# Attention of a decoder layer: the causal steps of all head groups first, then the context steps

## The reference

```
for each of 4 batches:
    x1  = x + mamba(norm(x))                       # a scan over 512 steps, 512 channels, 16 states
    xn  = norm(x1)
    q, k, v = xn Wq, xn Wk, xn Wv                  # 16 heads of 16 channels
    cq, ck, cv = xn Wcq, ctx Wck, ctx Wcv
    y   = softmax(mask(q k^T) / 4) v               # causal: 512 queries, 512 keys
        + softmax(cq ck^T / 4) cv                  # context: 512 queries, 1024 keys
    x2  = x1 + y Wp
    out = x2 + mixture_of_experts(norm(x2))        # 8 experts, 2 of them per token, and a gate
```

## Time and profile before

| | us |
|---|---|
| median of three runs (lowest, highest) | 1807.3 (1805.04, 1811.45) |
| the profiled execution, its own time | 1806.43 |
| its span, first to last instruction | 1804.6 |
| PE busy in the span | 1459.6 (81%) |
| DVE busy | 1285.0 (71%) |
| ACT busy | 818.7 (45%) |
| POOL busy | 645.6 (36%) |
| mean granted TensorE clock | 0.925 of 2.4 GHz |

### The profile page before, as it was taken

How to read it: one execution, slowest core, us unless ns; L and a number is a source line. 1 busy time by engine, 2 the same in 40 slices (tenths; PEclk the granted TensorE clock), 3 DMA queues, 4 the chain that set the end, 5 groups by cost and what they waited for, 6 DMA issues and landing times. The chain is left out here.

```text
span 1804.6 us, 19456 instructions
## 1 busy us (share of the span) xinstructions
PE 1459.6 (81%) x6520; PEld 720.5 (40%) x6520; DVE 1285.0 (71%) x2029; ACT 818.7 (45%) x1586; POOL 645.6 (36%) x630
## 2 busy tenths in 40 slices
PE   5697879995987799877887899945677998589995
PEld 2353522242544232243543222422242223378784
DVE  5998488748996778389985886599948881543324
ACT  3643336756443256664433467453323665222221
POOL 2565341303864322207653322056634021212130
PEclk9899979997999889998998899979997998689998
DMA  4950362003002532021004420030034302157744
GB/s 120 343 159 1 105 138 57 14 13 130 19 1 56 143 67 49 14 94 55 1 10 127 107 58 26 2 132 10 0 95 104 67 26 84 49 160 248 237 153 140
DMA packets 128068, 153.87 MB, mean 85 GB/s; under 512 B 19109, under 2 KB 107694, under 8 KB 125920
## 3 DMA queue, kind: packets, MB, share of 16 engines
q1 hardware_dynamic: 124224, 143.96, 27.5%
q0 software_dynamic: 3744, 8.66, 1.3%
HBM read 102.82 MB, written 50.99 MB: 85 GB/s over the span
## 5 line engine op out<-in xcount | busy, mean ns | idle before, releaser
L170 PE MATMUL PS<-arena 128*32 128x512 f32 (+10 forms) x4150 | 832.0, 450 | 85.0 <-DVE maxs L1849 21.5
L170 PEld LDWEIGHTS PS<-arena 128*32 128x32 f32 (+3 forms) x4150 | 363.9, 128 | 525.4 <-ACT arena L1821 205.6
L1821 ACT ACTIVATE arena<-PS 128x512 f32<-128x512 f32 (+3 forms) x768 | 361.6, 547 | 226.5 <-PE PS L170 225.5
L1404 POOL TENSOR_TENSOR arena<-arena 128x1024 f32<-128x1024 f32 x124 | 292.7, 2362 | 215.6 <-DVE arena L1429 117.1
L1849 DVE TENSOR_REDUCE maxs<-PS 128x1 f32<-128x1024 f32 x256 | 298.0, 1215 | 42.1 <-PE PS L170 41.9
L1429 DVE TENSOR_TENSOR_SCAN arena<-PS,arena 128x1024 f32<-128x1024 f32 x128 | 292.1, 2282 | 0.1
L170 PE MATMUL PS<-arena,ident 128*128 128x512 f32 (+1 forms) x560 | 256.5, 584 | 5.4 <-DVE arena L1438 5.4
L1376 ACT ACTIVATE PS<-arena,A_neg 128x511 f32<-128x511 f32 x256 | 165.9, 681 | 202.8 <-DVE arena L1429 202.6
L1438 DVE TENSOR_TENSOR arena<-arena,PS 128x1024 f32<-128x1024 f32 x128 | 156.3, 1221 | 6.8 <-PE PS L170 2.7
L1565 POOL TENSOR_SCALAR_AFFINE_SELECT arena<-arena 128x128 f32<-128x128 f32 x256 | 73.0, 296 | 235.9 <-ACT arena L1821 232.3
L170 PE MATMUL PS<-bc,bc_sel 96*128 96x512 bf16 x128 | 51.8, 405 | 118.8 <-DVE arena L1438 112.4
(11 more groups left out here) (264 smaller groups left out, 1549.7 us busy)
## 6 DMA issues: line engine op xcount, KB each, us to landing
arena<-in_ew SPq DMA_DIRECT2D x46, 512.0 KB
arena<-stack_parts SPq DMA_DIRECT2D x288, 64.0 KB, 2.3
rows_in<-nil SPq DMA_DIRECT2D x16, 1088.0 KB, 12.6
arena<-b_rows SPq DMA_DIRECT2D x16, 1024.0 KB, 7.7
stack_parts<-arena SPq DMA_DIRECT2D x40, 384.0 KB, 2.6
arena<-stack_parts SPq DMA_DIRECT2D x96, 128.0 KB, 4.3
arena<-rows_in SPq DMA_DIRECT2D x23, 272.0 KB, 5.3
xn<-dens SPq DMA_DIRECT2D x24, 256.0 KB
```

The costliest lines, as they stand in the source:

```text
L170: return nc.tensor.matmul(o, l, r, start=start, stop=stop)
L1404: nc.gpsimd.tensor_tensor(b_sb[i % 2], u[:, 2 * kh:2 * kh + 2, :], Brow[:, n, :].unsqueeze(1).to_broadcast([P, 2, T]), ALU.mult).then_inc( ...
L1821: nc.scalar.activation(probs[(HG * s + h) % NPR][:, 0:N], ring_bank(n)[:, 0:N], ACT.Exp, scale=HD ** -0.5).then_inc(S["ring_read"], 1)
```

## The change

The step order becomes side by side instead of group by group: steps 0 to 15 are the four causal steps of groups 0 to 3, steps 16 to 47 the eight context steps of groups 0 to 3.

- The job list is one list of 96 with the order: 8 causal jobs of group 0, 4 context jobs of group 0, then the causal jobs of groups 1, 2 and 3, the other 12 context jobs of group 0, and the context jobs of groups 1, 2, 3. Sixteen stand ahead of the first step; the table gives 2 or 3 per step up to step 10 and 2 per step from there until the list is empty. `TURNS` is the order of the turns: four causal, four context.
- `project(6)` and `project(7)` move ahead of the first job; they stood between the first jobs.
- Q and K are kept for all four groups (`q_last` is new), and SP loads them early. Loads, maximum rows and stores are written in a new order on SP.
- The causal `values` alternate between banks 6 and 7; so the score ring has two banks (4, 5) up to the first context step, and three from there.
- POOL writes the ones of K[0], K[1], K[2] and KC[0] before `low(2)`, where it wrote K[0] and KC[0]; K[3] and KC[1] before the first mask, KC[2] behind the last.
- The causal sides of all groups are copied to `YT[g]`, their denominators inverted once for all groups behind the parts of context group 1, and multiplied by POOL; the context sides follow group by group in `YX`, each inverted behind the parts of a later group.
- In `entry` the last group has only its context side left: 4 matrix multiplications in `turned_sums` and 4 in `spread_sums`, where 8 and 8 stood.

```diff
-            RING = (4, 5, 7)
-            TILE_BANKS = (0, 1, 6, 7, 4, 5, 6, 7, 6, 7)
+            TILE_BANKS = (0, 1, 6, 7, 4, 5, 6, 7, 4, 5)
+            PAIRED = HG * NG * TT + HG
+            def ring_bank(n):
+                return bank((4, 5)[n % 2] if n < PAIRED else (4, 5, 7)[(n - PAIRED) % 3])
+            def step(s):
+                return (s // TT, CAUSAL, s % TT) if s < NG * TT else \
+                    ((s - NG * TT) // CS, CONTEXT, (s - NG * TT) % CS)
+            TURNS = [(g, side) for side in range(2) for g in range(NG)]
...
-                JOBS_AT = [[0] * TT + [4, 2, 3, 3, 2, 2, 2, 2], [2] * STEPS, [2] * STEPS, [0] * STEPS]
+            JOBS_AT = [2, 2, 2, 3, 3, 2, 2, 2, 2, 3, 3] + [2] * (NSTEP - 11)
...
+                for s in range(NSTEP):
+                    g, side, k = step(s)
+                    if k == 0:
+                        pe.wait_ge(max_rows[g], 16 * 3 * (side + 1))
+                    pending = turned[0] < len(TURNS) and J > last_job(*TURNS[turned[0]])
+                    scores(s, (0, 1))
+                    if pending:
+                        max_rows_out(*TURNS[turned[0]])
+                    elif jobs:
+                        max_job(jobs[0])
+                    scores(s, (2, 3))
+                    if jobs and not pending:
+                        max_job(jobs[1])
+                    if s:
+                        values(s - 1)
+                    for j in jobs if pending else jobs[2:]:
+                        max_job(j)
...
                 def turned_sums():
                     pe.wait_ge(S["pv_copied"], 2 * NG)
-                    for i, y in enumerate(YS[(NG - 1) % 2]):
-                        for t in range(TT):
+                    for t in range(TT):
```

482 lines of the change are left out of this document (251 added, 231 removed).

## The result

The changed kernel takes **1794.8 us** (median of 6 executions, 1793.3 to 1796.3) against 1806.5 for the kernel before: a ratio of 0.9931, interval 0.9921 to 0.9942. Faster, then, by 12 us and not by the 28 that were forecast. Its profiled execution took 1793.6 us with a span of 1791.7, so it is compared with the 1806.4 and 1804.6 of before: -12.9 us of span.

What follows compares the result with a forecast made beforehand. PE and DVE were taken as the busy engines, each setting the pace in places. Start +3.3, exps -7.1 and tail -2.0 gave -5.8 for batches 1 to 3, -10.8 for batch 0: -28.2 from 1806.4, 1778 us, range 1765 to 1790.

Steps and rivals of the forecast that it cites:

- That is 17.8 us: From first job to first exp: reductions, turn, two rest, matrices, scores and exp were summed to 17.8 us.
- The 1.7 us of lower clock: Start of batches 1 to 3: a PE pause of about 3.5 us brings the lower clock, ending projections 1.7 us later.
- batch 1 speaks for all four: Attentions: exps take 147 us in both batches shown, so batch 1's trace was priced for all four.
- the 138.3 us of the sum: First to last exp step: causal block, context steps and turns sum to 138.3 us against 145.4 before, -7.1 us.
- the clock falls once more in the block: Rival, causal block: PE slack brings another lower-clock stretch, 3 to 5 us per batch, 1790 to 1798; chance 0.17.
- First job later by 3.3 us: Start of batches 1 to 3: two more K sets on POOL delay low(2) to (4), loads and first job by 3.3 us.
- Projections 6 and 7 in the gap: Start: PE does projections 6 and 7, 1.88 us each, while the first job waits for its loads, 4.17 us before.
- Causal block 50.3 us: Steps 0 to 15 with 36 jobs: groups of 12.0, 12.3, 13.6 and 11.9 plus 0.5 waiting, 50.3 us.
- The rival on the other side: Rival, steps 0 to 15: PE at 1.2 GHz through the causal block, about 22 us per batch, 1866; chance 0.10.
- A wait of 2.1 us for a stack in step 5: Causal step 5: group 3's Q and K loads queue behind maximum rows, PE waits 2.1 us, bounds 0 and 4.
- Steps of 2.89 and 2.45: Context steps: 2.89 us with two jobs (22 of them), 2.45 without jobs (nine intervals).
- Tail -2.0: Tail: two runs of 16 small matrix multiplications become 8 each, 2.0 us less on PE's way to the projections.

Runs made afterwards that it cites:

- experiment 4: Changed kernel with K[1], K[2] ones rows behind the low parts, rest(8), rest(9) among the first eight jobs, group 3 stacks loaded sooner: 1776.7 us, 0.9851.
- 7: experiment 4 with POOL's ones rows of K[3] moved behind the masks of step 4 and KC[1] behind the last mask: 1780.1 us, 0.9855.
- 11: 10 with three more idle multiplications per batch around the first turn: 1772.5 us, 0.9807.
- 10: 7 with one idle multiplication (result unread) per batch in PE's 1.06 us entry pause: 1773.6 us, 0.9819.
- experiment 3: Changed kernel with SP's loads of Q and K of group 3 issued ahead of the maximum rows of causal group 1: 1791.3 us, 0.9918.
- experiment 1: Changed kernel with POOL's ones rows of K[1] and K[2] set behind the low parts of tiles 2 to 4: 1787.5 us, 0.9912.
- experiment 9: Changed kernel with projections 6 to 9 put back behind jobs 1, 3, 5 and 7, their rest() between the maxima: 1806.8 us, 0.9989.
- Experiment 2: Changed kernel with rest(8) on DVE behind the maxima of jobs 0 to 3 and rest(9) behind jobs 4 and 5: 1798.8 us, 0.9947.
- experiment 13: Changed kernel with idle multiplications (results unread), one in the entry and three around the first turn per batch: 1794.2 us, 0.9918.
- Experiment 12: Kernel before with three idle multiplications (results unread) per batch around the turn of context group 0: 1791.2 us, 0.9917.
- 14: Kernel before with idle multiplications in the entry, around the first turn and at the turn of context group 0: 1801.4 us, 0.9966.
- 5: Changed kernel with one idle multiplication (result unread) per batch in PE's 1.06 us entry pause: 1794.7 us, 0.9925.
- 8: Kernel before with one idle multiplication (result unread) per batch in the entry: 1807.4 us, 1.0000.
- 15: 11 with one more idle multiplication, 384 columns wide, ahead of the multiplications that turn the denominators: 1769.0 us, 0.9799.
- experiment 6: Changed kernel with idle multiplications at four places per batch: entry, the 3.45 us pause, first turn, steps 10 and 11: 1794.7 us, 0.9935.

## Why the prediction was off

**The direction held, and of the mechanisms most; the size did not.** 1794.8 us lies within the 8-in-10 bounds (1757 to 1805) but outside the forecast's own range of 1765 to 1790. 15 us are missing, and two steps of the argument failed.

*The step "That is 17.8 us" (first job to first exp).* It takes 20.4 to 21.3 us, 2.6 to 3.5 us more in each of four batches; in batch 0, whose start was to be 1.7 us shorter, that made it 0.9 longer. In batch 1 (20.75) the pieces of the sum against the trace: the first matrix before the first reduction 1.6 instead of 0.9; eight jobs 6.9 instead of 6.7; turn and parts 1.45 as summed; two `rest` 2.7 instead of 1.5, the chain DVE, ACT, DVE; four context jobs 4.6 as summed; from there to the first exp 3.45 instead of 2.5, at 1.2 GHz. I summed durations of DVE and left out what stands between them. Experiments 4 and 7 confirm the chain: with `rest` moved up the stretch is 18.9 to 19.6 us. Part of the rest is the clock: with idle multiplications around the first turn the stretch is about 1 us shorter (18.2 to 18.4 in 11, 18.8 to 19.5 in 10). The 1.7 us of lower clock that I added to each start fell as forecast in batches 1 and 2 but cost nothing, since the loads landed no sooner (experiment 3). Net: 8 us too short over four starts. Batch 3's start grew by 6.4 us where batch 1's grew by 4.7; there the clock fell sooner. The multiplications by `out_w` took 8.83 us (8.56 in the kernel before, 7.14 in batch 1 of both), the second value tiles 3.78, not 2.52, and PE reached its first job 2.4 us later than in batch 1. PE of batch 3 (`out_w` at 1311.37):
```profile
1337.27 3.78 PE L172 MATMUL PS<-wv,xT 128*128 128x256 f32 x8 [3.45 <-ACT arena L1823]
1340.85 3.14 PE L172 MATMUL PS<-xT,wq 128*128 128x512 f32 x4
```

*The step "batch 1 speaks for all four".* That held before, where from first to last exp every batch took 146.7 to 147.1 us. It does not hold after. From first to last exp step, batch 1 took the 138.3 us of the sum (610.86 to 749.16), and that is part luck: the causal block took 0.8 us less than summed and the context steps 0.8 more. Batches 0, 2 and 3 took 1.0 to 2.7 us more. In batch 2 step 10 holds a fall (5.07 us to the next where batch 1 has 3.53; 1.4 us with step 11, which is 0.2 shorter), step 5 waits 0.6 us longer for the stack, and a turn with a cast of 1.27 us beside POOL's normalising costs 0.7; in batch 3 step 5 waits 0.9 us longer; in batch 0 a fall in steps 10 and 11 again is 1.0 us, step 5 0.4, and the first two steps 0.6. The rival *the clock falls once more in the block* (1790 to 1798, 0.17) was the right kind: it came in two batches of four, at 1.0 and 1.4 us instead of 3 to 5. No rival held the fall in the entry, 4.7 us, a part of the program that the change does not touch. The last tail, 21.0 us before and 16.9 now, gave 2 us back beyond the 2.0 that were forecast: its multiplications by `wp` ran at the lower clock for longer in the kernel before (10.20 us, 8.95 now).

Point by point otherwise:
- *First job later by 3.3 us*: +3.4. (By its own terms, 3.5 less 0.28, it is 3.2; and sixteen reductions of 0.41 are 6.6 us, not 6.7. Neither matters.) The cause is POOL's sets: without them -3.0 (experiment 1).
- *Projections 6 and 7 in the gap*: right; undone, all of the gain goes (experiment 9).
- *Causal block 50.3 us*: 49.5 in batch 1 (610.86 to 660.34), with errors that cancel. Group 2, eight context jobs, 14.2 (13.6); group 0 11.7 (12.0), group 1 11.35 (12.3), group 3 12.2 (11.9). PE was not at 1.2 GHz through the block: 1.00 from 616 on. The rival on the other side did not come.
- *A wait of 2.1 us for a stack in step 5*: 0 to 0.9 (0.4, 0, 0.6 and 0.9). My chain of SP's issues was right in kind, but PE came later than I had it: in batch 1 its first job of group 3 started at 627.84 with no wait at all, behind loads issued from 619.8 to 625.8.
- *Steps of 2.89 and 2.45*: right. Ten steps have no jobs; seven of the nine intervals between them are 2.46 us, as before, two 2.6:
```profile
736.88 2.07 ACT L1864 ACTIVATE arena<-PS 128x512 f32<-128x512 f32 x4 [0.39 <-PE PS L172]
...
749.16 2.06 ACT L1864 ACTIVATE arena<-PS 128x512 f32<-128x512 f32 x4 [0.39 <-PE PS L172]
```
- *Tail -2.0*: -2.1. PE of batch 1, for the earlier trace rows:
```profile
753.21 1.03 PE L172 MATMUL PS<-den_sel,arena 128*128 128x4 f32 x8 [0.87 <-ACT arena L1854]
...
755.05 1.16 PE L172 MATMUL PS<-ident,xn 128*128 128x128 f32 x8
```
- *The cast is slow beside a memory set and fast without*: the changed kernel's first cast takes 0.21 us with POOL idle; 1.13 and 1.24 us in experiments 2 and 4, ending with the set; 0.22 again in 7, where the set was moved. That is what the Trainium skill says (SBUF — State Buffer, "SBUF: two separate sides", the exclusive lock of VectorE and GpSimd), and these runs agree. For a VectorE instruction with two SBUF inputs the Trainium skill, in the same section, keeps the lock to GpSimd work that reads SBUF. These runs agree there too: the subtraction `mrest` - `mparts` takes 0.28 us beside a running set (experiments 2 and 4) and 2.33 beside an addition (experiment 13). But my step "now only short masks stand beside the turns" was wrong: POOL's normalisation and `x1 + bp` stand beside turns of the context groups (0.41 us for the cast in batch 1, 1.27 in batch 2, 0.58 in batch 3).
- *What pays*: the forecast named the lonely turn and the half-clock stretch together. Experiment 12 parts them: the stretch alone is 2.3 to 3.3 us per batch, 12.3 in all, of the 22.6 that the change brings between first and last exp.

**How much of the 15 us is the clock?** By the table and the steps: the entry 4.7, the falls in steps 10 and 11 2.4, batch 3's start 1.7, less 2.1 for the last tail: 6.7, a little under half. The mis-sized start is 6.5 more, and about 1 us a batch of that is the lower clock around the first turn; so the clock has 7 to 11 us, by this estimate. Stack waits and a slow cast are 2.7, the first steps of batch 0 0.6, and the other tails and the rest of the program give 1.3 back. These are readings of one execution; a separate experiment to settle the share (13 against 14) failed. **Open** is what decides where the clock falls. The same pause of 1.06 us in the entry was followed by a fall in 11 of 27 entries without the idle multiplication (none of 3 in the kernel before) and in none of 24 with it.

## What to carry to other kernels

A gain forecast from one batch's trace should be priced again for the clock: list the pauses of TensorE that the change makes, moves or removes, also behind it, where it only shifts the start of untouched code. A few idle multiplications in a pause that is surely idle are a cheap test, and can be worth as much as a reordering (here 16 us against 12, with intervals that overlap), but each must be judged by the whole time, since a fall prevented in one place can come back in another. And in a start-up stretch, sum the chain through all the engines, not the durations of the busiest one: `rest`, `middle`, `high`, `rest` in series, and POOL's memory sets ahead of what everyone waits for, cost more here than the moved loads.

## What the runs showed of the hardware

- *The lower clock after a short pause is not certain.* Behind the pause of 3.45 us ahead of value tile 10 it came in 12 of 18 batches (changed kernel, experiments 2, 3, 5, 9, 13), behind the same place's pause of 1.39 us in none of 24 (kernel before, experiments 1, 4, 7, 8, 10, 11, 15). Behind 1.06 us in the entry it came in 11 of 27.
- *Executions of one kernel follow their mean granted clock, roughly.* Experiment 2: 1785.5 us at 0.934, 1795.2 at 0.924, 1803.5 at 0.922, but 1800.6 at 0.928; experiment 4: 1775.6 to 1779.7 at 0.932 to 0.935, 1789.4 at 0.924. Experiments 1, 2 and 4 scatter by 14 to 18 us, the kernel before by 5 to 10, the changed kernel by 3. A mean clock that is higher by idle multiplications says nothing: 0.941 in experiment 6 at the changed kernel's time.
- *Code that no edit touches moves by some 4 us.* The experts at the end of the program took 265.2 to 269.7 us in the seventeen traces, and batch 0's start took 55.0 us in the kernel before and 53.4 in experiment 12, ahead of that run's first edit. A difference of a few us between two traces is not read as the edit's before these places are compared.
- *A set of 3 partitions on POOL holds up DVE's cast until it ends* (0.21 us becomes 1.13 to 1.51), *but not the subtraction behind it*, which kept its 0.28 us beside the next set in the kernel before and experiments 2, 4 and 12. An addition or multiplication on POOL holds up both (the cast 1.27 beside 1.28, the subtraction 2.33 beside 2.34). Reductions that read PSUM beside the same sets kept their 0.41 and 1.2 us.
